# Output projection of the first attention moved into its own stream, k ahead of q in the window attention, reordered front of the scan

## The reference

```python
def _L0_attn_ref(x, W_attn, b_attn, W_proj, b_proj):      # x: 4 sequences of 1024 tokens, 256 wide, 16 heads of 16
    qkv = x @ W_attn + b_attn
    ...
    att = jnp.einsum('bhtd,bhsd->bhts', q, k) / jnp.sqrt(jnp.asarray(D, x.dtype))
    att = att + _alibi_causal_mask(T, H, x.dtype)[None]
    att = jax.nn.softmax(att, axis=-1)
    y = jnp.einsum('bhts,bhsd->bhtd', att, v)
    y = y.transpose(0, 2, 1, 3).reshape(B, T, C)
    return y @ W_proj + b_proj
...
def _layer(x, wqkv, qs, ksc, wo, lg, lb, w1, b1, w2, b2):  # twice
    h = shift_token(x)
    qkv = h @ wqkv                                         # 8 heads of 64
    ...
    q = l2norm(q) * qs
    k = l2norm(k) * ksc
    q, k = rotary_xpos(q, k)
    o = local_attention(q, k, v)                           # windows of 128 tokens, each sees itself and the one before
    x = x + o @ wo
    ...
...
x = x + _L0_attn_ref(_layernorm(x, axis=-1), ...)
x = x + _L0_ffn_ref(_layernorm(x, axis=-1), ...)
x = x + _L1_attn_ref(_layernorm(x, axis=-1), ...)
```

## Time and profile before

| | us |
|---|---|
| three runs | 3927.00, 3919.38, 3925.37, median 3925.37 |
| the profiled execution | 3929.91, of which the span is 3928.1 |
| A | 0 to 140 |
| B | 140 to 697 |
| C | 698 to 768 |
| D, first layer / second layer | 772 to about 1350 / 1645 to about 2251 |
| F | 2514 to 2845 |

### The profile page before, as it was taken

One profiled execution on the slowest core, in us unless ns is written; L12 is line 12 of the kernel. 1 busy time (PEld: TensorE's weight loads), 2 busy tenths in 40 slices (PEclk: granted clock), 3 DMA queues, 4 the chain that ended last, 5 costly groups with the idle time before them and its releaser, 6 DMA issues. The chain is left out here.

```text
span 3928.1 us, 51446 instructions
## 1 busy us (share of the span) xinstructions
PE 3315.6 (84%) x18352; PEld 1997.2 (51%) x18352; DVE 2446.8 (62%) x3414; ACT 1837.8 (47%) x3892; POOL 1531.3 (39%) x970
## 2 busy tenths in 40 slices
PE   8599999488989889789898799799378888888894
PEld 4244443345555545455555555433155655556773
DVE  8488886456565522155656433268589999996533
ACT  2178788145555511155555411145467777773100
POOL 4100000233333311133333221135499999995503
PEclk9699999799999989999999999899699999999897
DMA  5946650610000041100000032133355251413573
GB/s 160 146 60 73 73 72 12 206 32 18 21 18 21 12 142 49 65 14 21 18 21 18 19 103 64 56 115 141 120 205 181 85 191 54 188 54 124 180 218 118
DMA packets 282792, 342.57 MB, mean 87 GB/s; under 512 B 71556, under 2 KB 217836, under 8 KB 281900
## 3 DMA queue, kind: packets, MB, share of 16 engines
q1 hardware_dynamic: 268732, 315.54, 29.2%
q10 hardware_dynamic: 10736, 15.38, 1.2%
q0 software_dynamic: 3072, 8.39, 0.7%
HBM read 231.21 MB, written 107.48 MB: 86 GB/s over the span
## 5 line engine op out<-in xcount | busy, mean ns | idle before, releaser
L2330 POOL TENSOR_TENSOR H_feed<-H_ndu,H_bs 128x1024 f32<-128x1024 f32 x256 | 595.0, 2364 | 5.3 <-DMA H_bs<-between_bc 2.8
L709 ACT ACTIVATE B_probs<-B_p_exp,B_key_bias 128x512 f32<-128x512 f32 (+3 forms) x768 | 393.0, 582 | 109.0 <-PE B_p_exp L753 78.7
L643 DVE TENSOR_REDUCE B_part_max<-B_p_max 128x1 f32<-128x512 f32 (+3 forms) x768 | 375.4, 546 | 95.1 <-PE B_p_max L730 92.5
L1230 ACT ACTIVATE D_probs<-D_scores,D_neg,D_rq 128x256 f32<-128x256 f32 x512 | 281.6, 564 | 237.5 <-DVE D_neg L1148 237.5
L2301 ACT ACTIVATE H_decay<-H_ndt,H_rate 128x1024 f32<-128x1024 f32 x256 | 287.8, 1125 | 197.3 <-DVE H_turning L2383 102.8
L1089 POOL TENSOR_TENSOR D_rnorm<-D_norm,D_power 128x8 f32<-128x8 f32 x64 | 106.1, 1658 | 633.4 <-DVE D_norm L1107 633.4
L727 PE MATMUL B_p_max<-B_k,B_q 100*128 100x512 bf16 (+3 forms) x768 | 256.4, 340 | 40.0 <-DMA B_key_bias<-in_key_bias 34.1
L1644 PE MATMUL E_p_ag<-E_hT,E_w 128*128 128x512 f32 x640 | 284.7, 605 | 2.0 <-ACT E_hT L1600 2.0
L2383 DVE TENSOR_TENSOR_SCAN H_turning<-H_decay,H_feed 128x1024 f32<-128x1024 f32 x112 | 253.5, 2274 | 24.7 <-POOL H_feed L2330 21.9
L2434 PE MATMUL H_p_y<-H_minus,H_sT 128*128 128x128 f32 x1792 | 232.2, 286 | 35.7 <-ACT H_sT L2286 35.7
L2434 PEld LDWEIGHTS H_p_y<-H_minus,H_sT 128*128 128x128 f32 x1792 | 223.5, 199 | 75.7 <-ACT H_sT L2286 55.7
(11 more groups left out here) (265 smaller groups left out, 7056.4 us busy)
## 6 DMA issues: line engine op xcount, KB each, us to landing
H_bs<-between_bc SPq DMA_DIRECT2D x64, 512.0 KB, 7.3
H_cs<-between_bc SPq DMA_DIRECT2D x36, 512.0 KB, 7.9
B_q<-between_q_parts SPq DMA_DIRECT2D x96, 128.0 KB
B_k<-between_k_parts SPq DMA_DIRECT2D x96, 128.0 KB
D_base<-between_z SPq DMA_DIRECT2D x64, 128.0 KB
between_z<-D_z SPq DMA_DIRECT2D x64, 128.0 KB, 1.7
E_rest<-between_z SPq DMA_DIRECT2D x16, 512.0 KB, 5.5
between_sz<-F_sz SPq DMA_DIRECT2D x8, 1024.0 KB, 4.2
```

What stands on the lines that cost most here:

```text
L643: nc.vector.reduce_max(part_max[:, g % 2, kc, qb, h:h + 1], p_max[:, n % 3, 0:keys], AX.X).then_inc(maxed, 1)
L709: nc.scalar.activation(probs[:, x % PROBS, skip:512], p_exp[:, n % SCORES, skip:512], ACT.Exp, bias=key_bias[:, g % SETS, kb - 4 * Q + 4, ...
L1230: last = nc.scalar.activation(probs[:, place[m], :, :].rearrange("p a b -> p (a b)"), scores[:, place[m], :, :].rearrange("p a b -> p (a b ...
L2330: nc.gpsimd.tensor_tensor(feed[:, n % AHEAD, :], ndu[:, g % 2, :], bs[:, s, :], ALU.mult).then_inc(fed, 1)
```

## The change

Three parts, all of them in what stands where.

**B and C.** `phase_project` is gone. The projection is cut into 16 units of 256 tokens, `(i, j)`: sequence `i`, quarter `j`. Units (i, 0) and (i, 1) stand in PE's stream of group `4i + 3` at `e` = 38 and 43, units (i, 2) and (i, 3) in group `4i + 4`, the next sequence's first, at `e` = 34 and 40; the last sequence's (3, 2) and (3, 3) follow behind the stream. A unit is four matmuls into the next `p_max` bank; DVE adds x plus bias, takes statistics and normalises three places later; POOL adds the bias and makes the inverse deviation by a power. yT stays in SBUF: `store(f)` copies from tile to tile. SP also loads x and stores x1 and z inside B.

**D.** Squares, reduction, table products and PE's projection are done for k first and for q later, each in an instruction of half the width. q's sum moves from POOL to DVE. PE turns k ahead of q.

**F.** DVE takes the next statistics between the four `put_xin` and normalises ahead of its convolution. POOL makes the inverse deviation ahead of the series. ACT copies the turned xn ahead of the two xs that DVE convolved.

The core of the diff:

```diff
+        GROUP_OF = {0: (3, 38), 1: (3, 43), 2: (4, 34), 3: (4, 40)}
+        added_at = {(4 * i + back, e): (i, j) for i in range(SEQS) for j, (back, e) in GROUP_OF.items()
+                    if 4 * i + back < NG}
+        normal_at = {(g, e + 3): unit for (g, e), unit in added_at.items()}
+        tail_units = [(SEQS - 1, 2), (SEQS - 1, 3)]
...
                 for h in range(GH):
-                    at = (f // 2) * GW + HD * h
-                    sp.dma_start(T["yT"][at:at + HD, 512 * (f % 2):512 * (f % 2) + 512],
+                    at = g % 2 * GW + HD * h
+                    sp.dma_start(yT[at:at + HD, i % 2, g % GROUPS // 2, 512 * (f % 2):512 * (f % 2) + 512],
                                  yn[32 * h:32 * h + HD, f % 2, :]).then_inc(stored[f % 2], 16)
...
+            def project(unit):
+                i, j = unit
+                use = unit_use[unit]
+                pe.wait_ge(w_loaded, 32)
+                pe.wait_ge(stored[j // 2], 64 * GROUPS * (i + 1))
+                reached(pe, maxed, use - 2)
+                for t in range(2):
+                    at = (2 * j + t) * P
+                    for c in range(KD):
+                        last = nc.tensor.matmul(p_max[:, use % 3, t * DIM:(t + 1) * DIM], yT[:, i % 2, c, at:at + P], w[:, c, :],
+                                                start=c == 0, stop=c == KD - 1)
                 last.then_inc(scored, 1)
...
+            def add(unit):
+                i, j = unit
+                n, use, c = order_of(unit), unit_use[unit], 2 * i + j // 2
+                part = x[:, c % 2, j % 2 * 2:j % 2 * 2 + 2, :]
+                dve.wait_ge(scored, use + 1)
+                dve.wait_ge(biased, c + 1)
+                nc.vector.tensor_tensor(part, p_max[:, use % 3, :].rearrange("p (t d) -> p t d", t=2), part, ALU.add
+                                        ).then_inc(maxed, 1)
+                dve.drain().then_inc(x1_ready, 1)
+                for t in range(2):
+                    last = nc.vector.bn_stats(stats[:, t, :], part[:, t, :])
...
+            for unit in tail_units:
+                add(unit)
+            for unit in tail_units:
+                normalise(unit)
...
-                nc.gpsimd.tensor_tensor(qr[:, :, :], qka[:, 0, :, :], qkb[:, 0, :, :], ALU.add).then_inc(q_rotated, 1)
...
+            def sum_q(i):
+                reached(dve, qk_turned, i)
+                nc.vector.tensor_tensor(qr[:, :, :], qka[:, 0, :, :], qkb[:, 0, :, :], ALU.add).then_inc(q_rotated, 1)
...
                 exps(i, 0)
                 if i + 1 < TILES:
-                    squares(i + 1)
+                    squares(i + 1, 1)
                 exps(i, 1)
+                if i + 1 < TILES:
+                    squares(i + 1, 0)
...
-                for m in range(2):
+                for m in (1, 0):
                     for k in range(KD):
                         last = nc.tensor.matmul(p_qk[:, m, :], hT[:, i % 2, k, :],
                                                 wqkv[:, k, m * INNER:(m + 1) * INNER], start=k == 0, stop=k == KD - 1)
-                last.then_inc(qk_done, 1)
+                    last.then_inc(qk_done, 1)
...
-                if k >= 2:
-                    series(k - 2)
                 if k + 1 < K:
                     inverse(k + 1)
                 if k >= 2:
+                    series(k - 2)
                     inputs(k - 2)
...
                 if k + 1 < K:
                     put_xT(k + 1)
+                if k < K:
+                    put_xs_last(k)
```

More of the change, by code:

```diff
@@ L524, in phase_attention @@
         stored = [a.sem(f"stored_{b}") for b in range(2)]
+        w_loaded = a.sem("w_loaded")
+        x_loaded = [a.sem(f"x_loaded_{b}") for b in range(2)]
+        biased = a.sem("biased")
+        x1_ready = a.sem("x1_ready")
+        stats_ready = a.sem("stats_ready")
+        var_ready = a.sem("var_ready")
+        rstd_ready = a.sem("rstd_ready")
+        z_ready = a.sem("z_ready")
+        x1_stored = [a.sem(f"x1_stored_{b}") for b in range(2)]
+        z_stored = [a.sem(f"z_stored_{b}") for b in range(2)]
+        first_row = a.sem("first_row")
         LOADED = 16 * 17
@@ L546, in steps_done, with order_of @@
             return STEPS * (f // 2) + (FIRST if f % 2 == 0 else STEPS)
+        max_use, unit_use = {}, {}
+        for n in range(NM):
+            max_use[n] = n
+        for g in range(NG):
+            for e in range(NE):
+                for n in beside(g, e):
+                    max_use[n] = len(max_use) + len(unit_use)
+                if (g, e) in added_at:
+                    unit_use[added_at[g, e]] = len(max_use) + len(unit_use)
+        for unit in tail_units:
+            unit_use[unit] = len(max_use) + len(unit_use)
+        def order_of(unit):
+            return 4 * unit[0] + unit[1]
         @block.sync
@@ L682, in _ @@
                         maxima(m)
+                    if (g, e) in added_at:
+                        add(added_at[g, e])
+                    if (g, e) in normal_at:
+                        normalise(normal_at[g, e])
                     if e == 6 and g:
@@ L909 @@
+            for unit in tail_units:
+                project(unit)
 LH, LD, WIN = 8, 64, 128
@@ L1252, in _ @@
             put_hT(0)
-            squares(0)
+            squares(0, 1)
+            squares(0, 0)
             put_hT(1)
@@ L1946, in logs_second @@
                                                ALU.min, ALU.subtract).then_inc(ndt_ready, 1)
-            statistics(0)
+            statistics(0, range(CT))
+            variance(0)
             normalise(0)
@@ L1952, in _ @@
                 if k < K:
-                    for m in range(XT):
-                        put_xin(k, m)
+                    put_xin(k, 0)
+                    if k + 1 < K:
+                        statistics(k + 1, (0, 1))
+                    put_xin(k, 1)
+                    if k + 1 < K:
+                        statistics(k + 1, (2, 3))
+                        variance(k + 1)
+                    put_xin(k, 2)
+                    put_xin(k, 3)
+                    if k + 1 < K:
+                        normalise(k + 1)
                     if k == 0:
@@ L2004, in put_xs, with put_xs_last @@
                                          ).then_inc(xs_ready, 1)
+            def put_xs_last(k):
                 act.wait_ge(conv_ready, k + 1)
```

319 lines of the change are left out of this document (153 added, 166 removed).

## The result

The changed kernel takes 3813.54 us (median of four runs, 3812.43 to 3819.22) against 3926.18 us, a ratio of 0.9719 (95% interval 0.9703 to 0.9736): 112.6 us less, where 106 were forecast. Its profiled execution spans 3812.3 us, 115.8 less than before.

What follows compares the result with a forecast made beforehand. PE bounds B, no engine is full in C, D loops through PE's projection, ACT's square and DVE's chain, F through DVE and POOL. -30 - 64 - 12.5 = -106.5 from 3925.4: 3820 us, range 3785 to 3864.

Steps and rivals of the forecast that it cites:

- The tail's saving: Between B and D: C's 77.5 us go, a tail for units (3,2) and (3,3) stays; 62.6 us saved.
- The units in the stream: In B: 14 units add 24.2 us of matmuls and 8 us of bank waits, 32 us, ends 24 and 58.
- I take a quarter, 8 us: In B: PE's waits for p_max banks cost a quarter of the units' whole DVE time, 34 us.
- 4 to 5 that were to show it: In B: groups 3, 4, 7, 8, 11 and 12 would be 4 to 5 us longer than the others.
- The rival on B's banks: In B: DVE's additions hold PE for most of their length, 50 us added instead of 32, total 3838; chance 0.12.
- The wait for yT: In B: a unit at e = 38 has 3 us to spare, or is up to 7 us late; taken at nothing.
- the second pair of units in the next group has most of a group to spare: In B: units (i, 2) and (i, 3) come long after their yT lands, so no wait was counted.
- D: Window attention: period 16.83 us, 1.08 less a tile over 62 tiles; with layer starts -64 us, ends -37 and -77.
- The start of a layer: In D: q follows k with nothing beside it, about 1.7 us more per layer, 3.4 in all.
- The port: In D: by the skill's rule each DVE sum waits for what is left of POOL's power, some 0.4 us.
- The two rivals that made D dear: In D: sums wait for half of POOL's powers (3859, chance 0.18) or whole powers, DVE the bound (3966, chance 0.04).
- F: Front of the scan: period 33.6 to 31.6 us over five steps, 2.5 at the start; -12.5 us, ends 0 and -21.

Runs made afterwards that it cites:

- b_last_give: Changed kernel with unit (3,1)'s normalising behind the last transposition, its chunk's stores behind the last yT, POOL's last bias ahead of the inverses: 3821.38 us.
- b_normalise_pool: Changed kernel with reordered tail and the tail units' first channel half multiplied early, plus normalising of the thirteen stream units on POOL instead of DVE: 3808.34 us.
- part_two: Kernel before with only D changed (window attention in halves, k first): ratio 0.9805 (0.9776 to 0.9834).
- part_three: Kernel before with only F changed (reordered front of the scan): ratio 0.9981 (0.9966 to 0.9997).

## Why the prediction was right, and where it was not

The sum was -106, the measurement -113, and the order of the parts was right. That the two are so close is partly luck: B and C gave 7.9 us less than forecast, D 19.3 more, F 2.8 less. Term by term:

- **The tail's saving**, forecast 62.6: 61.0. The two units' matmuls took 6.55 us, not 4.8: the estimate was made at C's granted clock of 0.75, and in the tail it was 0.56 (734 to 741), behind 9.5 us in which PE had no work.
- **The units in the stream**, forecast 32 us: 40.7. From B's first issue to the last yT issue it is 573.2 us before and 611.4 after, 38.3 more, though the part ahead of the first shift write was 2.4 shorter. 12 units cost 32.9 of it, 2.7 each. In the last group it is 3.1 more up to the last `weigh`, for two units, and 3.2 more from there to the last yT issue, of which b_last_give took 2.6 back. The remaining 1.4 lie in the first two groups, which hold no unit, and differ from execution to execution (-0.3 to 1.4 against the kernel before). The failed step is "I take a quarter, 8 us": the price beyond the matmuls' 24.2 is 16.5 us, half of the upper bound. A group with two units grew by 5.4 us, above the 4 to 5 that were to show it. The rival on B's banks (50 us) lies on the far side of what was measured. Its mechanism, DVE holding PE by way of the banks, is seen at a smaller size: the waits end at DVE, and DVE's normalising is worth a third of the price.
- **The wait for yT**, taken at nothing: nothing was waited for, but "the second pair of units in the next group has most of a group to spare" was wrong. Its stores stand behind the loads of a later group on SP and take 9 to 11 us to land, and the third unit had 1.4 to 2.3 us to spare, less than the first (2.7 to 3.4). In b_normalise_pool a landing 1.8 us later used it up.
- **D**, forecast 16.83 us a tile: 16.65. The turning of probs started at 9.54, not 9.75: PE's last matmul ahead of it starts at 9.43 in both kernels, and the turning starts 0.11 us behind that, not behind its recorded end at 9.70, from which I counted. Both sums ran free, at the better end. The start of a layer was forecast 1.7 us longer; to the first score it was 1.5 and 1.8 us shorter (30.2 and 30.5 to 28.7 us). Two things stand in that. From the end of k's inverse norm to the first score it is 5.0 us before and 5.6 after: q behind k costs 0.6 us, not 1.7, and kr, which POOL's sum had stretched to 1.75 us there, takes 0.69. The sign comes from ahead of that, from POOL's table products, which start 1.8 and 2.4 us earlier. In part_two, where they don't, the first score is 1.3 and 0.2 us later than before. So the cost of the start was over-sized, and that the layer became shorter is not the work of this part. Of the 83.3 - 64 = 19.3 us that D gave beyond the forecast, the period explains 62 x 0.18 = 11 and the two starts 1.5 + 1.8 + 3.4 = 6.7, of which the earlier products are 4.2.
- **The port.** The rows of kr and of the convolution had shown that POOL holds DVE. The Trainium skill, "SBUF — State Buffer", section "Who interferes with whom", has the loser wait for the other's whole instruction. For xn beside poly and pick the trace agrees (8.18 us). For ksum and qr beside the 128x8 powers it does not: 0.69 us each, begun 0.45 us ahead of the end of a power of 1.66. There the measurement decides: the power on 8 elements a partition did not hold either sum. The two rivals that made D dear had their chances from taking it for an operation like POOL's sum.
- **F**, forecast -12.5: -9.7 in this pair of executions, and -7.5 by the ratio of part_three. The size came out near for a wrong reason. I took 33.6 us as the period of five steps; only two had it, and the earlier trace rows show one of these, with PE's projection at a granted clock of 0.70. The step that failed is reading a period from one step without looking at its neighbours and at PE's clock in it. Against the short step the new one is 0.8 us longer, not 2.0 shorter, and part_two's F, in the old order without long steps, takes 317.1 us, as long as the new one. What the new order gives is about 4 us at the start, where 2.5 were forecast, and that it has no long steps.

## What to carry to other kernels

Before a period is multiplied, read it at every step of the phase, with PE's granted clock beside it: one slower projection made 33.6 us out of 30.9 here, and an unchanged function differed by 10 us between executions. A long elementwise operation on POOL can cost DVE its whole length. Here DVE's normalising, its convolution and its sums of two SBUF operands were held, while its statistics were not (0.74 us for two, inside POOL's 4.54 us ndu). So price such an operation on both engines, and see whether DVE does it in a fraction of the time. Work folded into a full engine's stream cost its own length and half as much again here (2.7 us for 1.8); what it leaves at the end of the stream is a chain of its own, in which anything written ahead of the last transfer is paid in full. An experiment that moves work to another engine must be read for the waits that it brings in, before its number is held against a bound.

## What was not expected of the hardware

The comparison of 128x2048 f32 to int32 took POOL 5.4 us and DVE 1.22. POOL's power on 128x8 did not delay a DVE addition of two SBUF operands that began inside it (0.69 us), while POOL's 128x512 sum stretched the same kind of operation from 0.68 to 1.58. In F an unchanged order of instructions ran in 317.1, 323.9 and 326.6 us in three kernels that differ only in other phases, and the steps that were longer had PE's projection late, at a granted clock of 0.70 to 0.83 in three of four. In B the same kind of store, 32 KB from tile to tile, landed in 2.4 us at the median and in 9 to 11 us where SP had issued a group's loads just ahead of it.
